# A relational graph layer on one core: node rows loaded and stored four per partition, from arrays that the host has laid out

## The reference

```
h   = relu(layernorm(x))                                   # 50000 x 128
W   = einsum('rb,bdf->rdf', w_comp, weight)                # one matrix per edge type
agg = segment_sum(h[src] * norm, etype * N + dst)
y   = einsum('rnd,rdf->nf', agg, W) + h_bias + h @ loop_weight
out = x + relu(y)
```

## Time and profile before

| what | us |
|---|---|
| median of 3 executions | 1160.69 |
| lowest, highest | 1157.90, 1162.27 |
| the profiled execution, its own time | 1159.61 |
| its span, first to last instruction | 1157.8 |
| granted TensorE clock, mean over the span | 0.99 of full |

### The profile page before, as it was taken

The page is one execution under the profiler, slowest core; times in us unless marked ns, Lnnn a source line. Parts: engine busy times, 40 slices in busy tenths (PEclk is TensorE's granted clock), DMA queues, the critical chain, the costliest instruction groups (busy, mean ns, idle before and its releaser), DMA issues. The chain is left out here.

```text
span 1157.8 us, 24700 instructions
## 1 busy us (share of the span) xinstructions
PE 1084.4 (94%) x5388; PEld 699.0 (60%) x5388; DVE 1036.0 (89%) x4391; ACT 942.8 (81%) x3334; POOL 810.1 (70%) x1387
## 2 busy tenths in 40 slices
PE   0399999999999999999999999999689999999997
PEld 0374444444444444444444444444289999999997
DVE  1429999999999999999999999999689999999995
ACT  0139999999999999999999999998468888888885
POOL 4018888888888888888888888886245555555553
PEclk9999999999999999999999999999889999999999
DMA  1102222222222222222222222221399999999993
GB/s 45 34 7 71 73 63 72 74 72 72 67 68 74 72 72 71 64 73 72 72 73 63 71 73 73 72 65 60 91 271 298 296 297 299 293 303 296 298 298 117
DMA packets 88393, 144.57 MB, mean 125 GB/s; under 512 B 17683, under 2 KB 56916, under 8 KB 88244
## 3 DMA queue, kind: packets, MB, share of 16 engines
q0 software_dynamic: 28224, 76.93, 22.8%
q1 hardware_dynamic: 60020, 66.07, 19.1%
HBM read 91.44 MB, written 51.49 MB: 123 GB/s over the span
## 5 line engine op out<-in xcount | busy, mean ns | idle before, releaser
L607 PE MATMUL y_ps<-w_all,hT 128*128 128x512 f32 x1568 | 704.6, 596 | 1.0 <-ACT hT L547 0.7
L607 PEld LDWEIGHTS y_ps<-w_all,hT 128*128 128x128 f32 x1568 | 284.1, 191 | 313.5 <-issue 287.7
L405 POOL DMA_INDIRECT xg<-x,idx x392 | 395.5, 1009 | 77.2 <-issue 50.0
L494 ACT ACTIVATE z<-y_ps,mix 128x128 f32<-128x128 f32 x784 | 245.3, 364 | 59.0 <-PE y_ps L607 52.1
L726 DVE SCALAR_TENSOR_TENSOR sum_b<-y_ps,mix,sum_b 128x128 f32<-128x128 f32 x784 | 266.5, 340 | 0.0
L381 POOL TENSOR_TENSOR u<-z 128x128 f32<-128x128 f32 x392 | 181.8, 464 | 76.2 <-ACT z L494 73.0
L443 POOL DMA_DIRECT2D out<-res x98 | 75.6, 771 | 131.7 <-DVE res L959 131.7
L726 DVE SCALAR_TENSOR_TENSOR sum_b<-y_ps,mix,z 128x128 f32<-128x128 f32 x392 | 137.1, 350 | 31.6 <-ACT z L490 9.7
L574 ACT ACTIVATE hw<-xw,shift,nrstd 128x128 f32<-128x128 f32 x392 | 161.5, 482 | 2.1 <-DVE shift L950 0.4
L661 PE MATMUL y_ps<-w_loop,hwT 128*128 128x128 f32 x782 | 152.4, 276 | 0.0
L662 PE MATMUL y_ps<-seg,pick 96*128 96x128 f32 x782 | 152.3, 276 | 0.0
(11 more groups left out here) (97 smaller groups left out, 1313.2 us busy)
## 6 DMA issues: line engine op xcount, KB each, us to landing
seg<-msgs SPq DMA_DIRECT2D x391, 96.8 KB, 4.0
msgs<-msg SPq DMA_DIRECT2D x98, 258.0 KB
xw<-x POOLq DMA_DIRECT2D x97, 256.0 KB, 5.9
out<-res POOLq DMA_DIRECT2D x97, 256.0 KB, 4.9
xg<-x,idx POOLq DMA_INDIRECT x392, 2.6
w_all<-L_gnn_weight SPq DMA_DIRECT2D x1, 512.0 KB, 5.3
src_all<-src SPq DMA_DIRECT2D x1, 194.5 KB
dst_i<-dst SPq DMA_DIRECT2D x1, 194.5 KB
```

The costliest lines, as they stand in the source:

```text
L405: nc.gpsimd.indirect_dma_start(xg[:, q, j, :], None, x, bass.IndirectOffsetOnAxis(ap=idx[:, q, j:j + 1], axis=0)).then_inc(s_gather[q * G ...
L494: ins = nc.scalar.activation(z[:, r, b, :], y_ps[r][:, b, :], ACT.Copy, scale=mix[:, q, j, b:b + 1])
L607: nc.tensor.matmul(y_ps[r][:, b0:b0 + B // 2, :], hT[:, q, j, :], w_all[:, b0:b0 + B // 2, :], start=True, stop=True).then_inc(done, 1)
```

## The change

The host makes a second copy of x, `x_rows`, padded with zeros to 98 x 512 rows and laid out as [98 groups, 128 partitions, 4 x 128 floats]: a partition's four rows of a group now lie behind one another, 2,048 bytes in one piece. The load of a group is one DMA from `x_rows[g]`. `out` has the same layout, a group's store is one DMA into `out[g]`, and the host puts the rows back in order. The gathers of the edge stage still read `x`. In the last group, the x load takes all four windows (the fourth is zeros) in one DMA instead of two, and the store takes three whole windows in one DMA instead of two.

```
-        X_WIN = x[0:(NW - 1) * P, :].rearrange("(w p) d -> p w d", p=P)
-        OUT_WIN = out[0:(NW - 1) * P, :].rearrange("(w p) d -> p w d", p=P)
-        LAST_FULL = NW - 1 - (NGW - 1) * G
+        LAST_WINDOWS = NW - (NGW - 1) * G
...
-            def store_results(g, q, full=G, last=0):
+            def store_results(g, q, windows=G):
                 r = q % NRING
                 pool.wait_ge(n_res, g + 1)
-                if full:
-                    pool.dma_start(OUT_WIN[:, bass.ds(g * G, full), :], res[:, r, 0:full, :]).then_inc(n_out[r], 16)
-                if last:
-                    pool.dma_start(out[(NW - 1) * P:N, :], res[0:last, r, full, :]).then_inc(n_out[r], 16)
-
-            def load_x(g, n, q, full=G, last=0):
+                pool.dma_start(out[g, :, 0:windows * F], res[:, r, 0:windows, :].rearrange("p j f -> p (j f)")
+                               ).then_inc(n_out[r], 16)
+
+            def load_x(g, n, q):
                 if not is_before(g, LRING):
                     store_results(g - LRING, q)
-                if full:
-                    pool.dma_start(xw[:, q, 0:full, :], X_WIN[:, bass.ds(g * G, full), :]).then_inc(n_x[q], 16)
-                if last:
-                    pool.dma_start(xw[0:last, q, full, :], x[(NW - 1) * P:N, :]).then_inc(n_x[q], 16)
+                pool.dma_start(xw[:, q, :, :].rearrange("p j d -> p (j d)"), x_rows[g, :, :]).then_inc(n_x[q], 16)
...
+    give("x_rows", x_rows.reshape(groups, G, P, D).transpose(0, 2, 1, 3).reshape(groups, P, G * D))
...
+    args.append(nc.dram_tensor("out", (groups, P, G * D), F32, kind="ExternalOutput").ap())
```

More of the change, by code:

```diff
@@ L66, in is_before, with build_layer @@
     return isinstance(g, int) and g < n
-def build_layer(nc, x, src, dst, etype, norm, weight, w_comp, loop_weight, bias, out):
+def build_layer(nc, x, x_rows, src, dst, etype, norm, weight, w_comp, loop_weight, bias, out):
     N, D = x.shape
@@ L79, in build_layer @@
     NW = -(-N // P)
-    LAST = N - (NW - 1) * P
     NGW = -(-NW // G)
@@ L345, in _, with load_windows @@
                     hold(sp, passed["sp"])
-            def load_windows(g, n, q, full=G, last=0):
+            def load_windows(g, n, q, windows=G):
                 if not is_before(g, LRING):
                     sp.wait_ge(n_res, g - (LRING - 1))
-                windows = full + (last > 0)
                 _, rows = nc.values_load_multi_w_load_instructions(
@@ L362, in _ @@
             g = NGW - 1
-            load_windows(g, g // LRING, g % LRING, LAST_FULL, LAST)
+            load_windows(g, g // LRING, g % LRING, LAST_WINDOWS)
         @block.gpsimd
@@ L470, in _ @@
             last_g = NGW - 1
-            load_x(last_g, last_g // LRING, last_g % LRING, LAST_FULL, LAST)
+            load_x(last_g, last_g // LRING, last_g % LRING)
             for g in range(NGW - LRING, last_g):
@@ L474, in _ @@
                 if ahead < NGW:
-                    relative(ahead, ahead // LRING, ahead % LRING, G if ahead < last_g else LAST_FULL + 1)
+                    relative(ahead, ahead // LRING, ahead % LRING, G if ahead < last_g else LAST_WINDOWS)
                 store_results(g, g % NRING)
-            store_results(last_g, last_g % NRING, LAST_FULL, LAST)
+            store_results(last_g, last_g % NRING, LAST_WINDOWS)
             for r in range(NRING):
-                pool.wait_ge(n_out[r], 16 * (len(range(r, NGW, NRING)) + (r == last_g % NRING and LAST_FULL > 0)))
+                pool.wait_ge(n_out[r], 16 * len(range(r, NGW, NRING)))
         @block.scalar
@@ L679, in _ @@
             g = NGW - 1
-            window_sums(g, g % LRING, LAST_FULL + 1)
+            window_sums(g, g % LRING, LAST_WINDOWS)
         @block.vector
@@ L912, in _, with window_stats @@
                     nc.vector.tensor_tensor(ccur[:, 0:F], ccur[:, 0:F], mix_ps[:, 0:F], ALU.add).then_inc(c_new, 1)
-            def window_stats(g, n, q, tiles, x_loads=1):
+            def window_stats(g, n, q, tiles):
                 r = q % NRING
                 if 0 in tiles:
-                    dve.wait_ge(n_x[q], n * 16 + 16 * x_loads)
+                    dve.wait_ge(n_x[q], n * 16 + 16)
                 for j in tiles:
@@ L961, in results, with node_step @@
                                                op1=ALU.add).then_inc(n_res, 1)
-            def node_step(g, n, q, windows=G, x_loads=1):
+            def node_step(g, n, q, windows=G):
                 ahead, ahead_n, ahead_q = g + 1, round_after(n, q, LRING), (q + 1) % LRING
-                window_stats(ahead, ahead_n, ahead_q, range(0, 1), x_loads)
+                window_stats(ahead, ahead_n, ahead_q, range(0, 1))
                 if not is_before(g, 2):
@@ L986, in _ @@
             g = NGW - 2
-            node_step(g, g // LRING, g % LRING, LAST_FULL + 1, 1 + (LAST_FULL > 0))
+            node_step(g, g // LRING, g % LRING, LAST_WINDOWS)
             window_shift(NGW - 1, (NGW - 1) % LRING)
@@ L991, in _ @@
             g = NGW - 1
-            results(g, g // LRING, g % LRING, LAST_FULL + 1)
+            results(g, g // LRING, g % LRING, LAST_WINDOWS)
 _INS = ["x", "src", "dst", "edge_type_32", "edge_weight1", "L0_gnn_weight", "L0_gnn_w_comp", "L0_gnn_loop_weight",
@@ L1004, with give @@
     arrays, args = {}, []
-    for name in _INS:
-        a = np.ascontiguousarray(inputs[name])
-        arrays[name] = a
-        args.append(nc.dram_tensor(name, a.shape, mybir.dt.from_np(a.dtype), kind="ExternalInput").ap())
-    args.append(nc.dram_tensor("out", inputs["x"].shape, F32, kind="ExternalOutput").ap())
+    def give(name, a):
+        arrays[name] = np.ascontiguousarray(a)
+        args.append(nc.dram_tensor(name, arrays[name].shape, mybir.dt.from_np(arrays[name].dtype),
+                                   kind="ExternalInput").ap())
+    x = inputs["x"]
+    N, D = x.shape
+    groups = -(-N // (P * G))
+    x_rows = np.zeros((groups * G * P, D), x.dtype)
+    x_rows[0:N] = x
+    give("x", x)
+    give("x_rows", x_rows.reshape(groups, G, P, D).transpose(0, 2, 1, 3).reshape(groups, P, G * D))
+    for name in _INS[1:]:
+        give(name, inputs[name])
+    args.append(nc.dram_tensor("out", (groups, P, G * D), F32, kind="ExternalOutput").ap())
     build_layer(nc, *args)
     r = run_bass_kernel_spmd(nc, [arrays], core_ids=[0])
-    return r.results[0]["out"]
+    out = np.asarray(r.results[0]["out"])
+    return out.reshape(groups, P, G, D).transpose(0, 2, 1, 3).reshape(groups * G * P, D)[0:N]
```

## The result

The changed kernel takes 1165.21 us (median of 10 executions, 1163.67 to 1167.04) against 1160.35 for the kernel before (10 executions, 1157.26 to 1162.78). The ratio is 1.0042, interval 1.0029 to 1.0055: 4.9 us slower, and clear of chance, though under the 0.5% that I had named as the bound of what can be told. The prediction was 1160.2 with a range up to 1163.5. In one later experiment (the kernel before with 8 more DMAs) one of ten executions took 1470.81 us at a granted clock of 0.85; its median and ratio are given without it.

The account below looks back on a forecast made before the run. TensorE, busy 100%, was taken to bound the node stage, so steady groups gave 0; -0.3 us at its start and -0.2 in the last group took the median from 1160.69 to 1160.2 us, range 1157.5 to 1163.

Parts of the forecast that it names:

- The pace: Steady node stage: TensorE, busy 100%, sets a pitch of 3.12 us per group, not the DMA engines.
- the term of the 94 steady groups: Steady node stage: 0.28 us less DMA time per group, covered by TensorE at 100%, so 0 us.
- The price of a long piece: Node-stage loads and stores: 2 KB pieces cost 42.3 engine-us per MB, against 50.9 for 512-byte rows.
- GpSimd's issue: Node stage: issuing a 128-piece DMA takes GpSimd 0.60 us, 0.16 less each, hidden in its idle time.
- The last store: Last group: one 192 KB DMA issued at 1152.79 lands at 1155.1 instead of 1155.28; -0.2 us, bounds -0.3 and +0.2.
- The forecast's -0.3 us at the start of the node stage: Before TensorE's transposes of group 2: messages land earlier behind cheaper x loads; -0.3 us, bounds 0 and -2.1.
- my -0.5: Whole kernel: sum of -0.3 us at the node stage's start and -0.2 us in the last group.
- the last group: End of the node stage: one store DMA in place of two lands sooner; term -0.2 us, bounds -0.3 and +0.2.
- The rival I named for slower, DMA as the bound: Steady node stage: at 10% more per byte, DMA takes 3.36 us a group, 22.6 us in all, 1183; chance 0.05.

## Why the prediction was wrong

**What was right.** The pace: TensorE at 100%, the term of the 94 steady groups 0. The price of a long piece came out in part. In the crowd the queue's share gives 0.504 x 16 x 200 / 33.63 = 48.0 engine-us per MB, against 50.9 before; I had said 42.3. For the last four stores, nearly alone (1146 to 1165.2 us), it is 0.134 x 16 x 19.2 / 0.98 = 42, as I had it from the message stores:

```profile
q0 software_dynamic: 304, 0.98, 13.4%
```

The Trainium skill, "DMA: Bandwidth & Descriptors", section Specifications, sees line rate from 512 bytes on. The trace again disagrees: 52.9 goes to 42 by longer pieces.

GpSimd's issue fell to 0.54 to 0.56 us (said 0.60). The last store: from the last matmul's start to the landing 1156.65 - 1153.27 = 3.38 us, before 1155.28 - 1151.51 = 3.77; I had said -0.2 with a bound of -0.3, it is -0.4. Here 1151.51 is the start of the last matmul in the trace of before:

```profile
1151.51 0.39 PE L664 MATMUL y_ps<-seg,pick 97*128 97x128 f32 x2
```

**What can't be told.** The forecast's -0.3 us at the start of the node stage drown in scatter: the second transposes stand at 855.19 and 853.50 in two profiles of one kernel. From the medians, 4.86 - 6.04 = -1.2 us are left for everything but the DRAIN, while the two kernels with stores from SyncE differ by 0.2; my -0.5 lies between.

**The step that failed** is the last group in "The change part by part". Its term was -0.2 us, and it followed the last store to its landing, 1155.28, and took what lies behind that up to 1157.8 and beyond for fixed, without a reason. In those 2.5 us stood a DRAIN of 2.03 us, which the view by source line would have shown, and it belonged to the very engine whose DMAs the change touches. It went to 8.07: a term of +6.0 us that the sum had at nothing. I costed what a DMA of fewer pieces saves at issue and in the DMA engines and never asked what else goes by their number: what is left for the end. The rival I named for slower, DMA as the bound, had nothing to do with it; the steady stage has no wait for DMA with the change either.

**What stays open.** That the DRAIN carries the loss is shown: four edits that leave the steady stage nearly as it is (the last eight stores short, a DRAIN under cover, stores from SyncE, 12 idle DMAs) each take 5 to 8 us away. That the DRAIN at the end costs 0.082 us for each DMA of 128 pieces since a DRAIN rests on two points, 5 and 46; by it the 8.07 us would stand for some 98 DMAs, where 83 lie behind the last gap. That GpSimd clears its books in the DRAIN and in the gaps is my reading; what happens inside either, what sets the place of a gap and what it leaves behind are not shown. Nor is it clear where 1.1 us of the kernel with 1,024-byte pieces are.

## What to carry to other kernels

Ask of an edit to DMAs not only what it does to transfers but what the program's end does with them: look behind the last landing, at the closing instructions of each engine. If GpSimd issues many DMAs, let its program end early (the last stores from another queue), or put a DRAIN where nothing due soon stands behind it; either gained 2.2 to 2.8 us here between medians on one chip (ratios 0.9972 to 0.9975), more than the 0.5 us I had forecast for the change itself. And a resource at a share of 1.03 that nobody waits for gives nothing when it is made cheaper.

## What the runs showed of the hardware

- GpSimd's DRAIN at the end took 0.46 us behind 5 light DMAs, 3.81 behind 46 (counted from a DRAIN before), and 8.07 at the end of the changed kernel, though all their data had landed and been waited for. It repeats to the nanosecond in two executions.
- GpSimd stops between two DMAs at counts that repeat from run to run: 1.1 us in the edge stage, 1.74 and 2.28 us in the changed kernel's node stage, 0.15 us every 16 DMAs with 512 pieces each. The DRAIN at the end was short where the last of these stops came late: 1.87 to 2.03 us with 2 to 8 DMAs behind it, 8.07 with 83.
- Adding 12 small DMAs to a kernel made it 6.1 us faster (1165.21 to 1159.09 on two chips; the ratio to the kernel before went from 1.0042 to 0.9990).
- A 256 KB store nearly alone cost 52.9 engine-us per MB in 512-byte pieces and 42 in 2,048-byte pieces; in the crowd of the node stage only 50.9 against 48.0.
